# Int8 weight scratch and one load queue replaced by bf16 scratch and loads alternating over two queues

## What is computed

```python
def fake_quant_weight(w, bits=8):
    qmax = 127
    scale = max(abs(w)) / qmax
    return clip(round(w / scale), -128, 127) * scale

def qat_lora_linear(x, W, b, A, B):
    return x @ fake_quant_weight(W).T + b + 2.0 * (x @ A.T) @ B.T

# attention block on LN(LN(x)): qk, v, gate = silu(x @ W.T + b); rope; attn; out = gate*(qo+lo) @ Wo.T
x = x + layernorm(attn_block(layernorm(x)))
h = gelu(qat_lora_linear(layernorm(x), W_fc, ...))      # 1024 -> 4096
x = x + layernorm(qat_lora_linear(h, W_proj, ...))      # 4096 -> 1024
```

## Time and profile before

| | us |
|---|---|
| the two runs | 2231.39 and 2296.65 |
| their median | 2264.02 |
| the profiled execution | 2231.54 |
| its span on the slowest core | 2230.0 (cores 2204.5 to 2230.0) |

### The profile page before, as it was taken

One profiled execution on the slowest core, in us unless ns is written; L12 is line 12 of the kernel. 1 busy time (PEld: TensorE's weight loads), 2 busy tenths in 40 slices (PEclk: granted clock), 3 DMA queues, 4 the chain that ended last, 5 costly groups with the idle time before them and its releaser, 6 DMA issues.

```text
span 2230.0 us, 17665 instructions; the slowest of 8 cores (2204.5 to 2230.0 us)
## 1 busy us (share of the span) xinstructions
PE 1206.4 (54%) x5596; PEld 530.3 (24%) x5596; DVE 856.2 (38%) x1374; ACT 326.4 (15%) x437; POOL 153.2 (7%) x240
## 2 busy tenths in 40 slices
PE   2101279951265166256526611788655561999955
PEld 0000146620122022122202200333211220333422
DVE  3333232043311412322141035898798445111344
ACT  0011212210111211111021010222000100222001
POOL 1000000000011011101101110011011000000000
PEclk9999989976589589768858965999878785999977
DMA  1111176125264255435435442454444221010222
GB/s 20 29 47 57 66 189 152 20 74 172 58 60 66 51 47 66 66 38 56 67 47 48 66 56 64 106 139 114 128 136 118 88 88 52 26 34 26 67 95 90
DMA packets 182483, 166.75 MB, mean 75 GB/s; under 512 B 83717, under 2 KB 149254, under 8 KB 182327
## 3 DMA queue, kind: packets, MB, share of 16 engines
q0 software_dynamic: 103392, 51.73, 18.7%
q1 hardware_dynamic: 79000, 113.90, 16.1%
HBM read 187.93 MB, written 20.97 MB: 94 GB/s over the span
## 4 chain that ended last, share of the span: by engine, by line
PE 36%; DVE 25%; DMA 19%; issue 11%; ACT 6%; DVEq 1%; POOL 0%; ACTq 0%; SPq 0%; POOLq 0%
PE PBIG L235 12%; PE PC L235 10%; PE PA L235 6%; DMA AW<-wgT 6%; DMA WSLB<-woT 6%; PE PD L235 4%; DVE FSCR L523 3%; DMA XT<-wpjT 3%; DVE FSC L527 3%; ACT AZQ L244 3%; DVE ST L366 2%; DVE ST L364 2%; DVE ISCR L520 2%; PE PD L232 2%; DMA XT<-x 2%
## 5 line engine op out<-in xcount | busy, mean ns | idle before, releaser
L235 PE MATMUL PBIG<-WSLB,AV 128*128 128x512 bf16 x512 | 145.1, 410 | 119.5 <-DVE WSLB L530 63.0
L235 PE MATMUL PBIG<-IDENT,AZQ 128*128 128x128 bf16 x192 | 30.6, 296 | 302.8 <-DVE AZQ L907 131.7
L235 PE MATMUL PC<-AY,AW 128*128 128x512 bf16 x252 | 100.0, 564 | 133.2 <-DMA AW<-wgT 104.9
L235 PE MATMUL PBIG<-AY,AW 128*128 128x512 bf16 x704 | 159.3, 379 | 17.0 <-DVE AW L530 15.0
L741 DVE TENSOR_TENSOR AGT<-PA,GATEE 128x512 bf16<-128x512 f32 x64 | 44.3, 692 | 295.5 <-PE PA L232 167.6
L485 DVE TENSOR_REDUCE MXP<-XT 128x1 f32<-128x1024 f32 x64 | 77.9, 1219 | 132.0 <-DMA XT<-wfcT 78.1
L235 PE MATMUL PBIG<-WSLB,AGT 128*128 128x512 bf16 x256 | 69.8, 397 | 97.8 <-DMA WSLB<-woT 93.2
L1034 DVE CAST WSLB<-ISCR 128x1024 bf16<-128x1024 int8 x96 | 66.3, 693 | 130.9 <-PE PD L232 107.8
L235 PE MATMUL PC<-QQ,QKK 128*128 128x128 bf16 x32 | 4.0, 306 | 189.9 <-ACT AZQ L244 113.6
L235 PEld LDWEIGHTS PBIG<-WSLB,AV 128*128 128x128 bf16 x512 | 49.3, 101 | 199.6 <-issue 152.2
L244 ACT ACT_TABLE_LOAD x15 | 19.2, 1283 | 511.9 <-DVE SA L1087 211.8
(11 more groups left out here) (232 smaller groups left out, 1944.5 us busy)
## 6 DMA issues: line engine op xcount, KB each, us to landing
XT<-wfcT SPq DMA_DIRECT2D x64, 512.0 KB, 4.1
XT<-wpjT SPq DMA_DIRECT2D x64, 512.0 KB, 4.0
AW<-wgT POOLq DMA_DIRECT2D x64, 256.0 KB, 4.7
WSLB<-woT POOLq DMA_DIRECT2D x64, 256.0 KB, 4.3
ISCR<-scr_pj SPq DMA_DIRECT2D x96, 128.0 KB, 2.0
XT<-x SPq DMA_DIRECT2D x16, 512.0 KB, 3.2
LKT<-scr_x SPq DMA_DIRECT2D x32, 256.0 KB, 3.1
AW<-wvT POOLq DMA_DIRECT2D x8, 512.0 KB, 7.2
```

What stands on the lines that cost most here:

```text
L235: e.matmul(o, a, b, start=s1, stop=s2))
```

## The change

The two scratch tensors become bf16. Their chunks are loaded straight into AW or WSLB, with no staging buffer and no cast on DVE; the load now waits for what the cast waited for. Chunks with even numbers are loaded on `sync`, those with odd numbers on `gpsimd`. The same alternation is put into `quant_max` and into `jit_quant`, whose stores stay on `gpsimd`. A switch read from the environment, off by default, would quantize every time instead.

```diff
-    sc_fc = nc.dram_tensor("scr_fc", [FF, D], I8, kind="Internal").ap()
+    sc_fc = nc.dram_tensor("scr_fc", [FF, D], BF16, kind="Internal").ap()
-    sc_pj = nc.dram_tensor("scr_pj", [FF, D], I8, kind="Internal").ap()
+    sc_pj = nc.dram_tensor("scr_pj", [FF, D], BF16, kind="Internal").ap()
...
 def quant_max(...):
-            ldt = dma("sync", stg, w2[:, c, j, :],
+            ldt = dma("sync" if b == 0 else "gpsimd", stg, w2[:, c, j, :],
                       deps=last(xtp[b]) + (list(start_deps) if i == 0 else []),
-                      ctr_name="qld")
+                      ctr_name="qld" if b == 0 else "qlg")
...
-    def jit_quant(st, b, w_src, wf, wf_deps, stt_dst):
+    def jit_quant(st, b, w_src, wf, wf_deps, stt_dst, store=True):
-        ldt = dma("sync", stg, w_src, deps=last(xtp[b]), ctr_name="qld")
+        ldt = dma("sync" if b == 0 else "gpsimd", stg, w_src,
+                  deps=last(xtp[b]), ctr_name="qld" if b == 0 else "qlg")
...
+        if not store:
+            return qf, None
         stt = dma("gpsimd", stt_dst, wf, deps=[qf], ctr_name="qst")
...
 fc, Cf == 1:
-                stg8 = ISCRI8[:, wb * 1024:(wb + 1) * 1024]
-                ld8 = dma("sync", stg8, scjA[o1],
-                          deps=last(wfc_cst[wb], q_fc["done"],
-                                    q_pj["done"], hl),
-                          ctr_name="wfl")
-                wdep = vop(lambda e, stg8=stg8, wb=wb: e.tensor_copy(
-                    out=AW[:, wb * 1024:(wb + 1) * 1024], in_=stg8),
-                    deps=last(ld8, wfc_prev[wb], wfc_st[wb]))
-                wfc_cst[wb] = wdep
+                wdep = dma("sync" if wb == 0 else "gpsimd",
+                           AW[:, wb * 1024:(wb + 1) * 1024], scjA[o1],
+                           deps=last(wfc_prev[wb], wfc_st[wb],
+                                     q_fc["done"]),
+                           ctr_name="wfl" if wb == 0 else "wfg")
...
 projection, the three later passes:
-                    ld8 = dma("sync", stg8, spj3[:, fc, :],
-                              deps=last(wpj_cst[wb], q_pj["done"], hl),
-                              ctr_name="wpl")
-                    wdep = vop(lambda e, stg8=stg8, wb=wb: e.tensor_copy(
-                        out=WSLB[:, wb * 1024:(wb + 1) * 1024], in_=stg8),
-                        deps=last(ld8, wpj_prev[wb], wpj_st[wb]))
-                    wpj_cst[wb] = wdep
+                    wdep = dma("sync" if wb == 0 else "gpsimd",
+                               WSLB[:, wb * 1024:(wb + 1) * 1024],
+                               spj3[:, fc, :],
+                               deps=last(wpj_prev[wb], wpj_st[wb],
+                                         q_pj["done"]),
+                               ctr_name="wpl" if wb == 0 else "wpg")
```

More of the change, by code:

```diff
@@ L146, in build_nc @@
     BFCTB = SIN[0:16, :]
-    ISCRI8 = ISCR.bitcast(I8)
     PBIG = nc.alloc_psum_tensor("PBIG", [128, 2048], F32)
@@ L171, in build_nc @@
                      "wfl0", "wfl1", "wpl0", "wpl1", "x2l0", "x2l1",
-                     "qst0", "qst1")}
+                     "qst0", "qst1", "wfg0", "wfg1", "wpg0", "wpg1",
+                     "qlg0", "qlg1")}
     pipetog = {}
@@ L945, in build_nc @@
         h_toks = []
+        import os as _os
+        _jit_all = _os.environ.get("KJIT_ALL") == "1"
         for o1 in range(NF):
             wb = o1 % 2
-            if Cf == 0:
+            if Cf == 0 or _jit_all:
                 wdep, stt = jit_quant(
@@ L952, in build_nc @@
                     last(wfc_prev[wb], wfc_st[wb], gt_free),
-                    scjA[o1])
-                wfc_st[wb] = stt
-            else:
-                stg8 = ISCRI8[:, wb * 1024:(wb + 1) * 1024]
-                ld8 = dma("sync", stg8, scjA[o1],
-                          deps=last(wfc_cst[wb], q_fc["done"],
-                                    q_pj["done"], hl),
-                          ctr_name="wfl")
-                wdep = vop(lambda e, stg8=stg8, wb=wb: e.tensor_copy(
-                    out=AW[:, wb * 1024:(wb + 1) * 1024], in_=stg8),
-                    deps=last(ld8, wfc_prev[wb], wfc_st[wb]))
-                wfc_cst[wb] = wdep
+                    scjA[o1], store=(Cf == 0))
+                if stt is not None:
+                    wfc_st[wb] = stt
+            else:
+                wdep = dma("sync" if wb == 0 else "gpsimd",
[3 more added lines that the diff above has]
+                           ctr_name="wfl" if wb == 0 else "wfg")
             ri = o1 % 3
@@ L1020, in build_nc @@
                 wb = fc % 2
-                if Cf == 0 and qp == 0:
+                if (Cf == 0 and qp == 0) or _jit_all:
                     wdep, stt = jit_quant(
@@ L1025, in build_nc @@
                         last(wpj_prev[wb], wpj_st[wb]),
-                        spj3[:, fc, :])
-                    wpj_st[wb] = stt
-                else:
-                    stg8 = ISCRI8[:, 2048 + wb * 1024:
-                                  2048 + (wb + 1) * 1024]
-                    ld8 = dma("sync", stg8, spj3[:, fc, :],
-                              deps=last(wpj_cst[wb], q_pj["done"], hl),
-                              ctr_name="wpl")
-                    wdep = vop(lambda e, stg8=stg8, wb=wb: e.tensor_copy(
-                        out=WSLB[:, wb * 1024:(wb + 1) * 1024], in_=stg8),
-                        deps=last(ld8, wpj_prev[wb], wpj_st[wb]))
-                    wpj_cst[wb] = wdep
+                        spj3[:, fc, :], store=(Cf == 0 and qp == 0))
+                    if stt is not None:
+                        wpj_st[wb] = stt
+                else:
+                    wdep = dma("sync" if wb == 0 else "gpsimd",
[4 more added lines that the diff above has]
+                               ctr_name="wpl" if wb == 0 else "wpg")
                 wdeps = last(wdep, h_done, t2_done) + \
```

## The result

The changed kernel takes 2623.72 us (median of 11 runs, 2612.23 to 2657.35), the kernel before 2234.08 us (median of 10). The ratio is 1.174, with a 95% interval from 1.170 to 1.178: 17% slower. 2640 was forecast. In some executions of either kernel one die shows a lower granted clock and the time is longer (2296.65 and 2292.59 us among the ten before); the ratios leave these out. The two profiled executions have spans of 2630.6 us on the slowest core (core 2) and 2230.0 us before (core 3), and all eight cores lie between 2590 and 2631 us, against 2204 to 2230 us.

A forecast was written before the change was run, and what follows sets the result against it. No engine bounds the whole kernel; the bound changes from stage to stage (PE, loads or DVE). Terms 80 + 7 + 96 + 90 + 21 + 115 = 409 us on 2231.5 give 2640 us, range 2530 to 2790.

The forecast's parts named there:

- V late: V product: its weight loads stand in POOL's queue behind 16 loads of the first maximum pass; +80 us, bounds +73 and +120.
- Second pass on POOL: Second maximum pass: POOL starts odd loads later than SP, 0.5 us a turn over 15 pairs; +7 us.
- fc and projection quantizing: Quantizing stages: odd loads stand behind stores on POOL and stall DVE, 6.0 and 5.6 us each; +96 and +90 us.
- Three projection passes: Projection reload: buffer turn of landing plus 2.6 us, 2.95 a chunk against 1.75; +115 us, bounds 67 and 182.
- fc reload: fc reload stage: 4.75 us a chunk against 4.08 for the matmuls, 32 chunks; +21 us, bounds 5 and 44.
- Casts: Reload stages: removing 128 DVE casts gains 0, since matmuls cover them; uncovered they would be 88 us.
- Queue order costs nothing: Rival: POOL passes waiting entries, V and quantizing keep their times, only 115 + 21 remain; 2368 us, chance 4%.
- Short landings: Rival: POOL loads without cast land in 3.2 us for 512 KB, 2.3 for 256 KB; 2520 us, chance 14%.
- Long landings: Rival: POOL loads land in 7.2 and 4.7 us, lengthening maximum passes, quantizing and reloads; 2900 us, chance 5%.
- Clock: Rival: PE idling drops its clock to 1.2 GHz in the reloads, adding 82 us projection, 60 fc; 2780 us, chance 7%.
- DVE relief: Rival: PE's gaps in reload stages are owed to casts; removing them takes up to 88 us off; 2144 us, chance 4%.

## Why the prediction was right

It put 409 us on 2231.5; the profiled executions differ by 400.6 us on the slowest cores and 400.5 on the mean core. By its own terms, against the mean core:

- **V late**: +80 forecast, V's first matmul +73.8 on the cores shown (+73.3 on the mean core), and V and second pass together +79.2 on the mean core (80 + 7 = 87 forecast). The lower bound, +73, was the better value: the V load took 9.1 us instead of 8, but went out at 361 and not 369, because the pass was shorter: 93.2 us on the mean core from its first to its last reduction, against 98.8 before and 99.0 in the run with its loads on SP, where V's loads run beside it again. That run gives back 71 to 76 us.
- **Second pass on POOL**: +7 forecast, +4.1 measured on the mean core (89.1 to 93.2 us from first to last reduction; 91.5 to 93.0 on the cores shown). The term took the same landing for both queues; in this pass the median over the cores is 4.2 us on POOL, 4.5 on SP beside it and 4.4 on SP before. That takes back a part of the 0.5 us by which POOL starts later: the term's sign was right and its size too large. The Trainium skill, page "DMA: Bandwidth & Descriptors", section "Rules for kernel authors", has it that spreading over issuing engines gives no bandwidth; the trace agrees, with 169 GB/s in this pass in either kernel.
- **fc and projection quantizing**: +96 and +90 forecast, +99.1 and +93.6 measured. The stall of an odd chunk is 99.1/16 = 6.2 us for fc and 93.6/16 = 5.9 for the projection, not 6.0 and 5.6, since the loads landed in 5.0 and 4.6 us and not in 4.7 and 4.3 as the nearest rows had it. The runs with loads one and two chunks ahead show the mechanism: what precedes the load in the queue.
- **Three projection passes**: +115 forecast, 34.1 + 66.2 = +100.3 measured. The landing is 2.9 us, 3.3 was taken; the other 2.6 us of the turn were right. 0.4 us less a turn is 0.2 a chunk, 96 x 0.2 = 19 us. Among the rows at hand, 2.3, 3.1 and 4.7, the middle one was nearest.
- **fc reload**: +21 forecast, +20.2 measured, but by luck in part: +15 with the direct reload alone, +17 on the six cores with full clock, and +29 on the two others. At full clock the term was too large for the reason of the term above: a landing of 2.9 us for 3.3 takes 0.2 off a chunk, 6 us in all, and 15 are left. The lower clock of two cores (last section), which the forecast didn't have, filled the gap.
- **Casts**: 0 forecast, 0 measured, shown by the run with four buffers: no casts, no gain.

The errors, -8, +3, +4, -15, -1, add up to -17; attention (+6) and the starts between stages make up for some of it. That the total came within 1% owes something to that, but no term was off by more than 15 us.

The rivals fell as follows. *Queue order costs nothing* (2368) is refuted by the runs in which the order alone changed: V loads first, one ahead, two ahead. *Short landings* (2520): half true for the reload, 2.9 us against 2.3 and 3.3, and wrong for the fp32 loads, which land in 4.6 to 5.0 in the quantizing stages (3.2 by that rival). An estimate by the Trainium skill, page "DMA: Bandwidth & Descriptors", section "Anatomy of one DMA — SWDGE (gpsimd) path", gave 2.6 and 3.2 us: the first is 0.3 under what the trace shows, the second 1.4 to 1.8, and the measured numbers decide. *Long landings* (2900) did not occur where that rival had them: 5.0 and 4.6 us against 7.2, and 2.9 against 4.7. *Clock* (2780): in the reload passes of the core shown the clock was 0.85 to 0.94; four matmuls took 1.21 us where it was 0.81 and 1.02 where it was full, in a turn of 5.9 against 5.5 us in the first pass, so the doubled matmuls of that rival never came. Its fc term, 60, is also too low by its own condition: the matmuls of a chunk would take 8.2 us each time, which alone is 3.4 more than the 4.75 forecast and gives 109. *DVE relief* (2144) is refuted by the direct reload alone (1.051) and by four buffers (1.002).

Do the parts add up? From the mean spans, the maximum passes cost 71.2, the quantizing loads 194.0 and the reload alone 120.2 us, together 385 of 400.5; 15 us are in none of them. Five of them are the fc reload, 160.3 us in the changed kernel and 155.3 with the direct reload alone, where no core needed more than 157.4; the rest was not traced.

## What to carry to other kernels

Before moving a DMA to another engine's queue, write out that queue in order and put beside each entry what it waits for: a load behind a store that waits for the consumer's last instruction is no prefetch any more, and costs its landing each time it comes round, while the same load written two chunks earlier cost next to nothing here (5 to 6 us a stage instead of 94 to 99). Before removing a staging copy, count what it gives: with a staging buffer "buffer free" to "buffer full" is one short cast, without it the whole issue and landing, unless there are enough buffers for the landing to hide. And take work off an engine only in stages where it ends last: 88 us of casts under matmuls were worth nothing, two of four instructions in two DVE-bound stages 3%.

## What was not expected of the hardware

On two of the eight cores of the changed kernel (2 and 3) the granted clock in the fc reload stage lay at 0.81 to 0.82 while the others had 0.97 to 1.00. The stretch 2212 to 2378 us of core 2 stands above; here it is on core 0:

```profile
2212.00:2378.00 166.00, 146.62 (x638) 56.69 (x637) 0.00 (x0) 41.18 (x35) 8.61 (x16) 0.99 0.17 51
```

Core 2's matmuls in the stage (tiles, count: duration ns smallest/median/largest, first and last start):

```profile
L235 PE MATMUL PBIG<-AY,AW x331: 378/437/438, 2211.7 to 2368.5; 128*128 128x512 bf16 x166
```

They take 379 ns in the kernel before. Two stretches of 10 us within the stage (2230 and 2300) had 0.81 as well, so this isn't one slow part in a fast whole: but for 6.5 us at full clock the record holds 0.81 throughout. The stage took 170 us there and 154 to 160 on the other six cores. In the run with the maximum passes on SP the same happened to cores 0 and 1 (0.85 and 0.86; 169 and 165 us), more weakly to cores 2 and 3 in the run with V loads first (0.91 and 0.90; 163 and 167 us) and to cores 0 and 1 in the run with the quantizing loads on SP (0.93 and 0.94; 163 and 160 us). In the run with the direct reload alone the stage took 154 to 157 us on all eight cores.

Over whole traces the picture is sharper. Stretches at 0.81 add up to 229 to 313 us on each of cores 0 to 3 of the changed kernel and to 0 on cores 4 to 7; to 0 on every core of the kernel before, though PE there is gapless for 130 us at full clock in the earlier trace rows; and to 0 in the run with loads two chunks ahead. It goes with the execution and not with the kernel: the mean clock of cores 0 to 3 was 0.78 to 0.79 in the profiled execution of the changed kernel and 0.80 to 0.81 in most of its others. So a stage of one profiled execution has to be compared over several cores, and with the clock beside it. What sets the level is open.

Also new: in the projection passes an SP load of a bf16 chunk from scratch lands in 2.6 to 2.7 us (median) when all loads are on SP, and in 2.8 to 2.9 when every other one is on POOL, while in the fc reload it is 2.6 to 2.7 either way; and DVE's multiply-and-add from f32 to f32 over 128x1024 takes 0.75 us and the add with bf16 output 0.69, where each instruction with two tensor inputs takes 1.22 to 1.28.
